# Differential attention: the output products of a batch split over the seam of two rounds, its gate and residual addition in the next round's first group, the next batch's normalization in the eighth group

## What is computed

```python
h = layernorm(x) * (1 + ca) + sa                       # ca, sa, ga: one row of 128 per batch
q1, q2, k1, k2 = heads(h @ Wq1), heads(h @ Wq2), heads(h @ Wk1), heads(h @ Wk2)
v = heads(h @ Wv)                                      # 16 heads of width 16
a1 = softmax(causal(q1 @ k1.T * scale)); a2 = softmax(causal(q2 @ k2.T * scale))
out = (a1 - lam * a2) @ v
out = (out - mean(out)) * rsqrt(var(out) + 1e-5) * (1 - LAM_INIT)
x = x + ga * (merge_heads(out) @ Wo)                   # merged: 256 channels, Wo: 256 x 128
```

## Time and profile before

| | |
|---|---|
| time, median of 3 runs | 1425.4 us (1425.11 to 1426.41) |
| the profiled execution's own time | 1424.91 us |
| its span, first to last instruction | 1423.2 us |
| PE, DVE, ACT busy, share of the span | 84%, 79%, 76% |
| mean granted TensorE clock | 0.933 of full speed |
| attention | from about 56 us to 663 us of the span |

### The profile page before, as it was taken

One profiled execution on the slowest core, in us unless ns is written; L12 is line 12 of the kernel. 1 busy time (PEld: TensorE's weight loads), 2 busy tenths in 40 slices (PEclk: granted clock), 3 DMA queues, 4 the chain that ended last, 5 costly groups with the idle time before them and its releaser, 6 DMA issues. The chain is left out here.

```text
span 1423.2 us, 25309 instructions
## 1 busy us (share of the span) xinstructions
PE 1195.5 (84%) x8837; PEld 561.8 (39%) x8837; DVE 1118.7 (79%) x1923; ACT 1080.7 (76%) x1727; POOL 834.0 (59%) x812
## 2 busy tenths in 40 slices
PE   4489999898989999885874778786669999999998
PEld 3234444444444444332553223232234444444443
DVE  5678878888888887876875998999947776787653
ACT  2178979798989797874976898896367888778775
POOL 3134646565656564540001798899637877778776
PEclk8589989999999999997998899999889999999999
DMA  5341414141414141100003799988578788877884
GB/s 138 101 133 53 143 36 141 41 140 43 146 36 146 42 141 46 48 2 1 0 1 96 249 308 312 302 288 290 180 158 190 180 194 191 197 179 180 193 204 118
DMA packets 123702, 198.79 MB, mean 140 GB/s; under 512 B 24604, under 2 KB 60088, under 8 KB 123576
## 3 DMA queue, kind: packets, MB, share of 16 engines
q1 hardware_dynamic: 122136, 195.08, 48.6%
q10 hardware_dynamic: 1440, 2.10, 0.5%
HBM read 167.76 MB, written 28.84 MB: 138 GB/s over the span
## 5 line engine op out<-in xcount | busy, mean ns | idle before, releaser
L1071 DVE TENSOR_REDUCE bmax<-p1b 128x4 f32<-128x512 f32 x640 | 405.7, 685 | 80.1 <-PE p1b L777 75.2
L698 ACT ACTIVATE pT<-p2b 128x512 f32<-128x512 f32 x640 | 349.7, 599 | 86.8 <-PE p2b L830 85.0
L2239 POOL TENSOR_TENSOR hid_l<-e_hid,w_experts 128x1024 f16<-128x1024 f32 (+1 forms) x136 | 281.9, 2084 | 97.8 <-ACT w_experts L2374 96.8
L2478 DVE TENSOR_TENSOR e_hid<-ub,w_experts 128x1024 f32<-128x1024 f32 x128 | 156.5, 1224 | 116.8 <-ACT ub L2385 104.7
L645 POOL TENSOR_SCALAR_AFFINE_SELECT pT<-pT 128x512 f32<-128x512 f32 (+1 forms) x192 | 148.5, 790 | 166.9 <-ACT pT L698 166.9
L848 PE MATMUL ob<-pT,vs 128*32 128x384 f32 (+3 forms) x2048 | 185.8, 450 | 8.9 <-ACT o_sb L704 6.9
L1940 PE MATMUL yb<-ch,ident 128*128 128x512 f32 x256 | 134.0, 654 | 42.9 <-POOL ch L1910 42.9
L2385 ACT ACTIVATE ub<-ub 128x1024 f32<-128x1024 f32 (+1 forms) x136 | 134.0, 985 | 41.3 <-PE ub L2290 39.6
L2374 ACT ACTIVATE w_experts<-e_hid 128x1024 f16<-128x1024 f32 (+1 forms) x136 | 139.4, 1026 | 28.1 <-DVE e_hid L2478 27.2
L777 PE MATMUL p1b<-w_high 48*128 48x128 bf16 (+2 forms) x1792 | 130.1, 248 | 26.4 <-DVE bmax L1071 26.3
L830 PE MATMUL p2b<-w_high 50*128 50x512 bf16 (+3 forms) x1024 | 125.8, 303 | 2.6 <-ACT pT L698 2.1
(11 more groups left out here) (315 smaller groups left out, 2158.6 us busy)
## 6 DMA issues: line engine op xcount, KB each, us to landing
w_experts<-shares SPq DMA_DIRECT2D x256, 256.0 KB, 4.6
brow<-bc_rows SPq DMA_DIRECT2D x64, 512.0 KB, 4.1
crow<-bc_rows SPq DMA_DIRECT2D x64, 512.0 KB, 5.1
q_stacks<-w_low SPq DMA_DIRECT2D x96, 128.0 KB
k_stacks<-w_low SPq DMA_DIRECT2D x96, 128.0 KB
w_high<-q_stacks SPq DMA_DIRECT2D x128, 96.0 KB, 2.3
w_high<-k_stacks SPq DMA_DIRECT2D x128, 96.0 KB, 2.3
w_high<-nparts SPq DMA_DIRECT2D x128, 4.0 KB
```

The source lines that it names most:

```text
L698: act.activation(pT[:, g2 % 2, stored(u), :], p2b[bank_of(g2, u)][:, :], ACT.Exp, scale=SCALE).then_inc(exp_done, 1)
L1071: dve.tensor_reduce(to, bank, AX, ALU.max).then_inc(first_read, 1)
L2239: pool.tensor_tensor(flat(hid_l[:, rounded(p), 0:n, :]), flat(hid[:, place(p), 0:n, :]), rounded_half(p, 0, n), ALU.subtract).then_inc(spl ...
L2478: dve.tensor_tensor(h, u, flat(share[:, p % SHARES, :, :]), ALU.mult).then_inc(hid_ready, 1)
```

## The change

The products with `Wo` are no longer one use of the bank in the eighth slot. Their first half (token tiles 0 and 1) is issued at the old place, the second half (2 and 3) in the next round's first slot, behind pair 0; `wo` is now the first use of that slot. The gate follows on DVE behind unit 2 of that slot (`GATE_AT`), the addition behind unit 6 (`ADD_AT`). Batch 7's products, gate and addition stay together in the last slot of round 8. The normalization of a batch moves from the first slot of a round, behind unit 0, to the eighth slot of the round before, behind unit 4 (`NORM_AT = 4`). ACT's `hT` moves from behind unit 2 to behind unit 3. In round 8 DVE collects the statistics of batches 0 to 5 first, then gates and adds batch 6, and then collects the rest.

```diff
@@ -442,11 +442,12 @@
 BANK_CREDITS = BANKS + (GROUPS * UNITS) % BANKS
 SCALE = 1.0 / math.sqrt(HD)
 DIAGONAL, EDGE, MIDDLE = "diagonal", "edge", "middle"
-AUX = {"project": 0, "turn_m0": 0, "turn_x": 1, "turn_m1": 1, "turn_neg": 2, "turn_o": 3, "value": 4, "wo": 5}
+AUX = {"wo": 0, "project": 0, "turn_m0": 0, "turn_x": 1, "turn_m1": 1, "turn_neg": 2, "turn_o": 3, "value": 4}
 CHUNKS = ((0, S), (P, S), (2 * P, S), (3 * P, S))
 CHUNK_FIRST, CHUNK_LAST = 1, 0
-O_COPY_AT, HIGH_AT, MT_AT, HT_AT, MID_AT, NEG_COPY_AT, OT_AT, V_COPY_AT = 0, 0, (1, 3), 2, 4, 4, 6, 9
-RES_AT, NORM_AT = 3, 0
+WO_FIRST, WO_LAST = (0, 1), (2, 3)
+O_COPY_AT, HIGH_AT, MT_AT, HT_AT, MID_AT, NEG_COPY_AT, OT_AT, V_COPY_AT = 0, 0, (1, 3), 3, 4, 4, 6, 9
+RES_AT, NORM_AT, GATE_AT, ADD_AT = 3, 4, 2, 6
 SQ_AT = 6
 RC_AT, SUM_AT, START_AT, MERGE_AT = (3, 9), (5, 9), (6, 1), (6, 6)
 MERGE_SCALE = (1.0 - LAM_INIT) ** -2
@@ -474,13 +475,13 @@
 
     kinds = ["turn_o", "turn_neg"]
     if g == 0:
-        kinds.append("turn_x")
+        kinds += ["turn_x", "wo"]
     if 1 <= g < 5:
         kinds.append("project")
     if 3 <= g < 7:
         kinds.append("value")
     if g == GROUPS - 1:
-        kinds += ["turn_m0", "turn_m1", "wo"]
+        kinds += ["turn_m0", "turn_m1"]
     return sorted(kinds, key=AUX.get)
 
 
@@ -732,7 +733,7 @@
                     if u in MT_AT and post and g == 7:
                         c = MT_AT.index(u)
                         act.wait_ge(aux_done, aux_use(r, g, f"turn_m{c}") + 1)
-                        act.wait_ge(aux_done, aux_use(r - 1, g, "wo") + 1)
+                        act.wait_ge(aux_done, aux_use(r, 0, "wo") + 1)
                         act.activation(mT[:, c, :], auxb[:, :], ACT.Copy).then_inc(aux_read, 1)
                     if u == V_COPY_AT and prep and 3 <= g < 7:
                         c = g - 3
@@ -853,6 +854,7 @@
             def slot(r, g, on, prep, post):
                 b, pb = r + 1, r - 1
                 late = not isinstance(r, int) or r >= 0
+                after = r >= 2
 
                 def aux_free(kind):
 
@@ -917,13 +919,20 @@
                         for i in range(TILES):
                             mm = pe.transpose(auxb[:, i * P:(i + 1) * P], merged[:, i, c * P:(c + 1) * P], k.ident[:, :])
                     if kind == "wo":
-                        if not post:
+                        if not after:
                             return skip(kind)
-                        aux_free(kind)
-                        for i in range(TILES):
+                        for i in WO_LAST:
                             for c in range(2):
                                 mm = pe.matmul(auxb[:, i * P:(i + 1) * P], mT[:, c, i * P:(i + 1) * P], k.wo[:, c, :], start=(c == 0), stop=(c == 1))
                     mm.then_inc(aux_done, 1)
+
+                def wo_first(n):
+
+                    pe.wait_ge(aux_read, aux_use(r + 1, 0, "wo"))
+                    for i in n:
+                        for c in range(2):
+                            mm = pe.matmul(auxb[:, i * P:(i + 1) * P], mT[:, c, i * P:(i + 1) * P], k.wo[:, c, :], start=(c == 0), stop=(c == 1))
+                    return mm
 
                 if isinstance(r, int) and (r, g) == (B, F_TURN_AT):
                     pe.wait_ge(f_xn, 1)
@@ -958,6 +967,8 @@
                         product(*lagged(r, g, 3), c)
 
                 pairs(0)
+                if g == 0:
+                    side("wo")
                 if 1 <= g < 5:
                     side("project")
                 if g == GROUPS - 1:
@@ -977,8 +988,11 @@
                 pairs(4)
                 if 3 <= g < 7:
                     side("value")
-                if g == GROUPS - 1:
-                    side("wo")
+                if g == GROUPS - 1 and post:
+                    if r == B:
+                        wo_first(range(TILES)).then_inc(aux_done, 1)
+                    else:
+                        wo_first(WO_FIRST)
                 weigh(0)
 
             rounds(pe, slot)
@@ -986,6 +1000,18 @@
         @block.vector
         def _(dve):
             fill = Chain(dve, dve_fill).link
+
+            def apply_gate(r, done):
+
+                dve.wait_ge(aux_done, aux_use(r, 0, "wo") + 1)
+                dve.tensor_tensor(gated[:, :, :], auxb[:, :].rearrange("p (c n) -> p c n", c=TILES),
+                                  k.gate_a0[:, done:done + 1, :].broadcast_to([P, TILES, D]), ALU.mult).then_inc(aux_read, 1)
+
+            def add_gated(r, done):
+
+                dve.wait_ge(aux_read, aux_use(r, 0, "wo") + 1)
+                x = k.x[:, done * TILES:(done + 1) * TILES, :]
+                dve.tensor_tensor(x, x, gated[:, :, :], ALU.add).then_inc(post_done, 1)
 
             def slot(r, g, on, prep, post):
                 b, pb = r + 1, r - 1
@@ -1006,9 +1032,13 @@
                         token_stats(dve, fill, k, range(1, B))
                 if isinstance(r, int) and r == B:
                     if g == 0:
+                        dve.wait_ge(post_done, B - 2)
+                        for n in range(B - 2):
+                            collect(dve, k, n)
+                        apply_gate(B, B - 2)
+                        add_gated(B, B - 2)
                         dve.wait_ge(post_done, B - 1)
-                        for n in range(B - 1):
-                            last = collect(dve, k, n)
+                        last = collect(dve, k, B - 2)
                         fill(last)
                     if g == 1:
                         finish_stats(dve, fill, k, range(B - 1))
@@ -1069,11 +1099,15 @@
                             to = bmax[:, g % 2, 2 * j:2 * j + 2, 14:17:SLOT_STEP]
                             bank = bank.rearrange("p (h c) t -> p h c t", h=2)
                         dve.tensor_reduce(to, bank, AX, ALU.max).then_inc(first_read, 1)
-                    if prep and (g, u) == (0, NORM_AT) and r >= 0:
-                        dve.wait_ge(aux_done, aux_use(r - 1, 0, "turn_x") + 1)
+                    if (g, u) == (GROUPS - 1, NORM_AT) and r + 2 < B:
+                        dve.wait_ge(aux_done, aux_use(r, 0, "turn_x") + 1)
                         for c in range(TILES):
-                            ins = normalize(dve, k, xn[:, c, :], b * TILES + c)
+                            ins = normalize(dve, k, xn[:, c, :], (b + 1) * TILES + c)
                         ins.then_inc(xn_ready, 1)
+                    if (g, u) == (0, GATE_AT) and 2 <= r < B:
+                        apply_gate(r, r - 2)
+                    if (g, u) == (0, ADD_AT) and 2 <= r < B:
+                        add_gated(r, r - 2)
                     if prep and u == RES_AT and 1 <= g < 5:
                         j, J = g - 1, b * 4 + g - 1
                         dve.wait_ge(hi_ready, J + 1)
@@ -1085,13 +1119,9 @@
                     whole = bmax[:, g % 2, :, :]
                     blocks = bass.AP(whole.tensor, whole.offset + 2, [whole.ap[0], [BLOCK_STEP, TILES], [MAP_WORDS, MAPS], [SLOT_STEP, BLOCK_SLOTS]])
                     dve.tensor_reduce(qneg[:, g % 2, :, :], blocks, AX, ALU.max, negate=True).then_inc(qneg_ready, 1)
-                if post and g == 7:
-                    dve.wait_ge(aux_done, aux_use(r, g, "wo") + 1)
-                    dve.tensor_tensor(gated[:, :, :], auxb[:, :].rearrange("p (c n) -> p c n", c=TILES),
-                                      k.gate_a0[:, bass.ds(pb, 1), :].broadcast_to([P, TILES, D]), ALU.mult).then_inc(aux_read, 1)
-                    dve.wait_ge(aux_read, aux_use(r, g, "wo") + 1)
-                    x = k.x[:, bass.ds(pb * TILES, TILES), :]
-                    dve.tensor_tensor(x, x, gated[:, :, :], ALU.add).then_inc(post_done, 1)
+                if isinstance(r, int) and (r, g) == (B, GROUPS - 1):
+                    apply_gate(B + 1, B - 1)
+                    add_gated(B + 1, B - 1)
 
             rounds(dve, slot)
```

## The result

The changed kernel takes 1435.5 us (median of 4 runs, 1434.3 to 1436.4), the kernel before 1425.3 beside it (4 runs, 1423.5 to 1426.4). The ratio, from runs paired on one chip, is 1.006 [1.0034, 1.0085], +8.6 us [4.9, 12.1]; the medians lie 10.2 apart. Repeated later against 25 runs of before it was +8.7 us, 1.0054 [1.0031, 1.0078]. The forecast was +6.0, 1431.4 us. The profiled execution took 1436.0 us, its span 1434.3, at a mean granted clock of 0.930. One of 29 later runs of the kernel before was in a slow state (1502.6 us at a granted clock of 0.808) and is left out of all medians.

What follows compares the result with a forecast made beforehand. It took PE as the engine with the least air in a full-clock round. Terms 4.0 + 0.9 - 0.4 + 0 + 1.5 gave +6.0 us, 1431.4 us; range 1426 to 1435, to 1437 with one more low stretch, down to 1425 with A.

Steps and rivals of the forecast that it cites:

- The sign: Whole kernel: slower than before, chance 0.77; same 0.15, faster 0.08.
- The seam: Seams 1/2 to 5/6: late normalization, gate and addition make PE wait, +0.8 each, +4.0 for five (1.5 to 5.5).
- the normalization's 1.33 start to start: Eighth slot: four normalizations take 1.33 us behind unit 4, delaying unit 6 and costing PE 0.88 at pair 4.
- Seam 0/1: Between rounds 0 and 1: the normalization enters the eighth slot and nothing leaves it, +0.9 us (0 to 1.0).
- Round 0: Its first slot: batch 1's normalization moves earlier, so turn_x stops waiting 0.41 for it, -0.4 us (-0.5 to 0).
- Seam 6/7: Between rounds 6 and 7: no normalization; PE's earlier start meets waits for DVE, 0 us (-0.5 to +0.4).
- Round 8: Last round: 24 bn_stats ahead of the gate delay PE's turn_x and pair 2, +1.5 us (0 to 2.5).
- A, hidden normalization: Eighth slot: DVE's idle 1.30 + 0.36 takes the normalization, sum +0.3, 1425.7 us; chance 0.12.
- B, the clock stays up: Rounds 1, 2, 6, 7: losing all four low-clock stretches gives -10, total -4, 1421.4 us; chance 0.10.
- C, more half-clock: New PE waits in the seam bring two more low-clock stretches of 6.6 us, +5, 1436.6 us; chance 0.15.

Runs made afterwards that it cites:

- e3: Changed kernel with the normalization back in the first slot behind unit 0; products, gate and addition as changed: 1433.8 us, +7.8 on the kernel before.
- e1: Changed kernel with the normalization behind unit 3 of the eighth slot instead of unit 4: 1432.8 us, +6.8 on the kernel before.
- e9: Repeat of e1, the changed kernel with the normalization behind unit 3: 1433.1 us, +6.0 on the kernel before.
- c1: The changed kernel again, unaltered, for a repeat and a second profile: 1436.1 us, +8.7 on the kernel before.
- c2: The kernel before again, unaltered, for a second profile: 1427.4 us in its one run.
- e2: Changed kernel with two batches' statistics instead of six ahead of round 8's gate: 1430.1 us, +4.2 on the kernel before.
- e8: Changed kernel with gate and addition behind units 1 and 3 instead of 2 and 6: 1430.6 us, +3.4 on the kernel before.
- e6: Kernel before with only the normalization moved, to the eighth slot behind unit 3: 1425.1 us, -2.3 on the kernel before.
- e5: Kernel before with only the normalization moved, to the eighth slot behind unit 4: 1432.2 us, +4.8 on the kernel before.
- e4: Changed kernel with normalization behind unit 3, gate behind 1, addition behind 3, two batches' statistics ahead of round 8's gate: 1421.1 us, -4.9 on the kernel before.
- e10: Repeat of e4, the changed kernel with those four places altered: 1423.6 us, -3.6 on the kernel before.
- e7: Changed kernel with normalization behind unit 3 and two batches' statistics ahead of round 8's gate: 1431.6 us, +4.4 on the kernel before.

## Why the prediction was right, and what it mis-sized

The sign and the path of every wait were right. The size +6.0 is close to what the slots add up to (+5.9) by luck in part: the terms of the seams 0/1 to 5/6 and of round 0 came out 1.3 us lower in all, those of round 8 and seam 6/7 1.2 higher. The measured +8.6 is more than either.

**The seam: mechanism right, size +0.64 for +0.8.** The first slot came out as worked: 9.33 us, for 9.35 (410.00 to 419.35). The eighth came out 10.04, for 10.23. The failed term is the normalization's 1.33 start to start, taken from its old place. In its new place it takes 1.02, so PE waits 0.55 and not 0.88; pair 4 comes 0.58 later in the slot and not 0.88. Behind it the slot is 0.89 shorter (3.52 to 2.63), where the forecast had 1.0, which takes a part of that away again.

The 0.31 between 1.33 and 1.02 has a row. In the old place the first of the four lasts 0.639 us, the others 0.33; in the new place all four last 0.34. The difference goes with what POOL does meanwhile. Its timeline in the kernel before, and then in `e3`:

```profile
411.31 0.64 POOL L645 TENSOR_SCALAR_AFFINE_SELECT pT<-pT 128x512 f32<-128x512 f32 x1
```

```profile
411.29 0.63 POOL L646 TENSOR_SCALAR_AFFINE_SELECT pT<-pT 128x512 f32<-128x512 f32 x1
```

Before, DVE's first normalization begins at 411.38 and ends at 412.02, 0.07 behind POOL's select (411.95). In `e3` it begins at 411.52, lasts 0.483 and ends at 412.00, 0.08 behind it (411.92): begun later, it is shorter by as much. In the new place POOL records nothing from 410.5 to 414. The seams 1/2, 2/3 and 3/4 of before show the same pair of instructions, 0.08 apart. One kernel shows both: in `e1` the normalization behind unit 3 meets no select and its first instruction lasts 0.34; in `e9`, the same kernel in another execution, it starts 0.21 into a select at the seams 1/2, 2/3, 3/4 and 5/6 and lasts 0.50, again until 0.08 behind it. The Trainium skill ("GPSIMD Engine Reference", "8. Key points") says that GpSimd shares its SBUF interfaces with VectorE and contends with some of its forms of instruction. These rows agree, with 0.31 us a time; no edit here moved the select alone, and no row says which form this instruction takes.

**Seam 0/1: +0.66 for +0.9**, by the same term (PE waits 0.69 there).

**Round 0: -0.7 for -0.4.** From its first pair to turn_x it takes 2.41 where it took 2.92. The whole slot takes 8.15 where it took 8.81, in every profile with the normalization in the eighth slot.

```profile
58.06 1.12 PE L898 MATMUL auxb<-ident,w_low 128*128 128x128 f32 x4
```

**Seam 6/7: +0.3 for 0.** The eighth slot gives 0.90 (9.46 for 10.36), and the first takes 1.18 (8.67 for 7.49), in `c1` and `c2`. The slots behind it are as before (7.47 for 7.48, 7.55 for 7.55), so nothing gives the 0.3 back. In the first slot PE waits 0.62 for the gate at the passed turn_x, so pair 2 starts 0.06 earlier than before, where the forecast had 0.5 left; at the slot's end it waits 0.28 for unit 8.

**Round 8: +2.4 for +1.5, the largest miss.** From DVE's last `qneg` to the last addition it lasted 43.17 and 42.67 us in the two profiles of before, and 44.6 to 46.0 (mean 45.4) in the six with this order of round 8. With two batches first it lasts 42.3 to 42.4, four times. So the order of round 8 is the cause, and `e2` against the changed kernel shows its price in the whole time, in separate batches: some 4 us (+4.2 against +8.6), with wide intervals. The delay of pair 2 itself was forecast well: it starts 5.78 us behind the last `qneg` where it started 4.37, +1.4 for +1.5. What the forecast left out is half clock behind the wait. In the changed profile pair 2 itself runs with 0.61 us matmuls where full clock gives 0.39 (above). In `c1` it begins within 1 us of it:

```profile
631.40 0.39 PE L831 MATMUL p2b<-w_high 50*128 50x512 bf16 x2 [2.34 <-PEq L869]
...
633.05 0.61 PE L831 MATMUL p2b<-w_high 50*128 50x384 bf16 x4
```

In `e1` the same wait is followed by full clock:

```profile
626.84 0.39 PE L831 MATMUL p2b<-w_high 50*128 50x512 bf16 x2 [2.33 <-PEq L869]
...
628.13 0.39 PE L831 MATMUL p2b<-w_high 50*128 50x384 bf16 x4
```

All six profiles with this order have the wait. Four (the changed kernel, `c1`, `e3`, `e9`) have 3.4 us at clock 0.50 right behind it; they take 45.4 to 46.0 us. Two (`e1`, `e8`) don't; both take 44.55, which is +1.6, the forecast's term. None of the eight profiles without the wait has half clock at this place. So the delay costs 1.6, and the half clock 0.9 to 1.4 more where it comes.

**The sum.** 5 x 0.64 + 0.66 - 0.7 + 0.3 + 2.4 = +5.9 us, against a forecast of 6.0: the seams' shortfall and round 8's excess cancel. The measured +8.6 and +8.7 stand above this; their intervals, [4.9, 12.1] and [4.4, 11.1], hold it. What the other 2.8 us are isn't settled.

The profiles bear the sum out. From the first slot of round 0 to the start of the last addition, less what the third and seventh slots of rounds 1 to 7 last above their shortest (8.05 and 9.82 us; 7.55 for the third of round 7), it takes 596.6 and 596.7 us in the two profiles of before, 603.8 and 602.1 in the two of the changed kernel: +6.3. What was taken off was 10.7 and 6.0 us before, 10.8 and 10.6 changed; it holds the half-clock stretches of the rounds.

In the two profiled executions the last addition of attention moved from 662.24 to 670.19, by 7.95, and the span by 11.1. Of the 7.95, 0.74 lie ahead of the first slot, which begins anywhere from 54.9 to 60.4 us in the fourteen profiles. The remaining 3.1 are not the change's. DVE's first and last scan of a later layer lie 238.6 us apart in the profile of before:

```profile
786.66 2.28 DVE L2086 TENSOR_TENSOR_SCAN gate_a<-dA,dBx 128x1024 f32<-128x1024 f32 x1
...
1025.29 2.29 DVE L2086 TENSOR_TENSOR_SCAN hs<-dA,dBx 128x1024 f32<-128x1024 f32 x1
```

In `c2`, the same kernel again, they lie 243.0 apart, as in the changed kernel (243.0) and `c1` (243.3):

```profile
785.34 2.28 DVE L2086 TENSOR_TENSOR_SCAN gate_a<-dA,dBx 128x1024 f32<-128x1024 f32 x1
...
1028.36 2.29 DVE L2086 TENSOR_TENSOR_SCAN hs<-dA,dBx 128x1024 f32<-128x1024 f32 x1
```

**The rivals.** A, hidden normalization, fell: PE waits 0.55. It would have held one unit earlier, as `e6` and `e1` show in their slots. B, the clock stays up, and C, more half-clock: the time at clock 0.50 from 90 us to the end of attention was 39.8 and 27.2 us in two executions of before, 40.0 and 41.0 in two of the changed kernel. Before spans almost the whole difference itself, so neither rival can be read from these sums. In one place C's mechanism is there: round 8's half clock behind the new wait. The mean granted clock over the timed runs was 0.9338 for `c1` and 0.9330 for before beside it: the clock explains nothing of its +8.7. Nor do the stretches belong to rounds 1, 2, 6 and 7, where the earlier trace rows had them: in `c2`, the same kernel, they are in rounds 1, 3 and 4.

**Open.** The same sum can be made for every kernel: five seams as in the table above, seam 0/1 (+0.66 with the normalization behind unit 4), round 0 (-0.7 with the normalization in the eighth slot), seam 6/7 (+0.3, or -0.5 with gate and addition early) and round 8 (+2.4, or -0.6 with two batches first). The last two are 0 in `e5` and `e6`. Against the measured medians (us, less before):

| kernel | slots and round 8 | measured |
|---|---|---|
| changed, `c1` | +5.9 | +8.7 |
| `e1`, `e9` | +2.4 | +6.8, +6.0 |
| `e2` | +2.9 | +4.2 |
| `e3` | +6.7 | +7.8 |
| `e4`, `e10` | -5.7 | -4.9, -3.6 |
| `e5` | +2.6 | +4.8 |
| `e6` | -0.9 | -2.3 |
| `e7` | -0.6 | +4.4 |
| `e8` | +0.8 | +3.4 |

All but `e6` measured 1 to 5 us above their sums, the most in `e7`, `e1` and `e9`. The mean granted clock over the timed runs was 0.9302, 0.9317 and 0.9321 in `e1`, `e9` and `e7` against 0.9343 and twice 0.9342 beside them; at -3.4 to -4.8 us for each +0.01 (below) that would be 1.0 to 2.0 us. A half-clock stretch in every round, as the profile of `e1` had it, was a possible cause; the profile of `e9`, the same kernel, has none in rounds 1 to 5. Some 2 us and more stay unexplained.

One wait that the forecast had no term for varies with the execution, in all kernels: at the end of the third slot PE waits for a transfer in some rounds. It adds 0 and 0.36 us to a whole execution in the two profiles of before, 0.71 and 0 in those of the changed kernel, at most 1.45 (`e9`). Here it is in `e2`, round 1, the longest single one:

```profile
154.94 0.39 PE L785 MATMUL p1b<-identb,later 64*128 64x256 bf16 x4 [0.96 <-DMA w_high<-k_stacks]
```

Whether the change makes it more frequent, fourteen profiles don't show.

## What to carry to other kernels

Splitting a block of PE work across a seam paid here only when what reads its result, and what was moved to make room, stood ahead of the first wait on PE that they could cause: one unit earlier for the normalization, one and three for gate and addition, and two batches of statistics instead of six ahead of round 8's gate turned +8.6 us into about -4. Work that is put into an in-order engine's idle time uses none of the idle ahead of the instruction it stands behind; find the idle time, then the unit in front of it. When the last round has its own order of work, price it by itself: here it cost nearly four times as much as a seam.

## What the runs showed of the hardware that was not expected

- DVE's normalization of a 128x128 f32 tile lasts 0.34 us with POOL idle, and 0.64 when it starts 0.07 into a POOL select of 0.64; started 0.21 to 0.24 into it, it lasts 0.47 to 0.50, and each of these ends 0.07 to 0.08 behind the select. Started 0.41 or 0.43 into it, it lasts 0.34 again. A duration read at one place isn't the duration at another.
- Stretches at half clock change their place from one execution of the same kernel to the next, and last 3.4, 6.8 or 10.2 us; one of 3.4 adds 1.3 to 1.8 us to the seventh slot of rounds 1 to 6. Over 25 timed runs of the kernel before, time goes with the mean granted clock (correlation -0.72; -0.68 over 28 runs of another batch, -0.54 over the 25 of the first, -0.81 over the 8 of `c1`), by about -4.8 us for +0.01 (-3.4 in the first batch). That goes with up to half of the variance of times that spread over 10 us.
- A wait of PE of 2.34 us was followed by 3.4 us at half clock in four of six executions, beginning within 1.6 us of its end, and by full clock in the other two.
- While the clock is full, a seam repeats to 0.01 us from round to round and from execution to execution. The slots resolve 0.04 us where the times can't tell 2 us from none.
